# State-space stage: skip term and residual additions in TensorE's open sums, copies on ScalarE, delta projection in two halves

## What is computed

```
x1  = layernorm(x + attn(x))                    # attn's last product: o @ wo
z   = x1
u   = silu(conv4(in_proj(ctx_1024)) + conv_b)   # (b, channel, t)
dt, Bm, Cm = split(x_proj(u))                   # 16, 16, 16 rows
delta = softplus(dt_proj(dt) + dt_proj_b)
for t: state = state * exp(delta_t * A) + (delta_t * u_t) * B_t ;  y_t = state . C_t
y   = (y + D * u) * silu(z)                     # D * u is the skip term
x2  = layernorm(x1 + y)
out = layernorm(x2 + ffn(x2))
```

## Time and profile before

| | |
|---|---|
| median of 3 runs | 4593.2 us (4591.05 to 4596.53) |
| the profiled execution's own time | 4590.23 us |
| its span, and mean granted TensorE clock | 4588.4 us, 0.957 |
| state-space stage's main loop | first scan 3086.0, last sum ends 3784.5 us |
| its tail | gate 3785.4, last x2 copy ends 3809.5 us |
| busy over the span | PE 4184.2, DVE 3306.2, ACT 2299.2, POOL 963.4 us |

### The profile page before, as it was taken

The page is one execution under the profiler, slowest core; times in us unless marked ns, Lnnn a source line. Parts: engine busy times, 40 slices in busy tenths (PEclk is TensorE's granted clock), DMA queues, the critical chain, the costliest instruction groups (busy, mean ns, idle before and its releaser), DMA issues. The chain is left out here.

```text
span 4588.4 us, 184268 instructions
## 1 busy us (share of the span) xinstructions
PE 4184.2 (91%) x76786; PEld 2616.5 (57%) x76786; DVE 3306.2 (72%) x5635; ACT 2299.2 (50%) x5544; POOL 963.4 (21%) x1800
## 2 busy tenths in 40 slices
PE   6899999999999999999999999859778777999999
PEld 4576666666666766666666766633333333444443
DVE  2788887888887887888888888739999992222211
ACT  2566666665666665666666666544353431111110
POOL 0333333332323232333333233200000000000000
PEclk9899999999999999999999999878889887999999
DMA  1211212121212122121212212123233323000000
GB/s 52 65 57 60 73 47 73 53 66 54 70 57 64 56 64 62 57 70 56 67 56 67 62 59 71 50 102 83 72 99 83 86 79 148 0 28 28 0 19 9
DMA packets 131632, 277.95 MB, mean 61 GB/s; under 512 B 20668, under 2 KB 62032, under 8 KB 127200
## 3 DMA queue, kind: packets, MB, share of 16 engines
q1 hardware_dynamic: 126176, 258.29, 18.4%
q10 hardware_dynamic: 4608, 7.60, 0.5%
HBM read 235.17 MB, written 30.67 MB: 58 GB/s over the span
## 5 line engine op out<-in xcount | busy, mean ns | idle before, releaser
L504 PE MATMUL a_pb<-a_x_t,a_w_qkv 128*128 128x512 f32 x1536 | 838.2, 638 | 12.6 <-DMA a_w_qkv<-in_w_qkv 12.1
L1176 DVE TENSOR_TENSOR a_nq<-a_nq,a_tot 128x512 f32<-128x512 f32 x768 | 509.6, 705 | 151.0 <-PE a_pb L526 101.5
L1152 DVE SCALAR_TENSOR_TENSOR a_acc<-a_pb,a_taps,a_acc 128x511 f32<-128x511 f32 (+2 forms) x576 | 425.0, 738 | 41.4 <-ACT a_acc L847 10.7
L1778 PE MATMUL m_p_y<-m_h,m_ident 128*128 128x512 f32 x512 | 292.4, 686 | 143.2 <-DVE m_h L1978 143.2
L526 PEld LDWEIGHTS a_pb<-a_nq,a_ks 128*32 128x32 f32 x20480 | 215.5, 112 | 213.1 <-issue 117.9
L2246 PE MATMUL f_pb<-f_x_t,f_w_gu 128*128 128x512 f32 x704 | 308.0, 592 | 0.0
L526 PE MATMUL a_pb<-a_nq,a_ks 128*32 128x32 f32 x20480 | 253.0, 201 | 49.2 <-DVE a_nq L1313 31.8
L1464 POOL COPY a_apt<-a_apt_fine 32x256 f32<-32x256 f32 x256 | 100.8, 394 | 936.9 <-DVE a_apt_fine L1197 912.1
L504 PEld LDWEIGHTS a_pb<-a_x_t,a_w_qkv 128*128 128x128 f32 x1536 | 239.7, 191 | 96.0 <-issue 59.7
L1972 DVE TENSOR_TENSOR_SCAN m_h<-m_da,m_h 128x2048 f32<-128x2048 f32 x64 | 283.1, 4424 | 5.9
L2300 ACT ACTIVATE f_gate<-f_pb 128x512 f32<-128x512 f32 x132 | 78.8, 597 | 410.9 <-PE f_pb L2246 274.6
(11 more groups left out here) (278 smaller groups left out, 9153.1 us busy)
## 6 DMA issues: line engine op xcount, KB each, us to landing
a_rows<-rows SPq DMA_DIRECT2D x192, 512.0 KB, 3.9
a_amp_sums<-amp_sums SPq DMA_DIRECT2D x64, 508.0 KB, 3.6
attn_o<-a_o_t SPq DMA_DIRECT2D x64, 256.0 KB, 2.6
m_b_rows<-ssm_bc SPq DMA_DIRECT2D x64, 256.0 KB, 3.7
m_c_rows<-ssm_bc SPq DMA_DIRECT2D x64, 256.0 KB, 4.6
m_o_t<-attn_o SPq DMA_DIRECT2D x14, 1024.0 KB, 8.6
a_w_qkv<-in_w_qkv SPq DMA_DIRECT2D x51, 256.0 KB, 3.0
f_w_gu<-in_w_gu SPq DMA_DIRECT2D x3, 1536.0 KB, 17.9
```

The lines of the kernel that those rows point to most:

```text
L504: mm = nc.tensor.matmul(pb[:, V_BANK if i == P_V else KQ_BANK], w_qkv[:, i, k], x_t[:, k, b * T:(b + 1) * T], start=(k == 0), stop=(k == D ...
L1152: last = nc.vector.scalar_tensor_tensor(acc[:, i, d:T], src[:, 0:T - d], taps[:, i, 3 - d:4 - d], acc[:, i, d:T], ALU.mult, ALU.add)
L1176: last = nc.vector.tensor_tensor(part, part, spread(blocks, shape), ALU.mult)
L1778: nc.tensor.matmul(p_y[:, et], ident[:], h[:, (b * DS + n) % 3, et], start=(n == 0), stop=(n == DS - 1), skip_group_check=True).then_inc(s ...
```

## The change

1. Skip term: `finish` is gone. Four 128x128 diagonal matrices `diag_d` are built once (`build_diag`, VectorE, batch 0, step 1). Each tile of `p_y` is opened by a product diag_d x u, and the state sums are added to it. `gate` reads p_y itself, so p_y may be opened for the next batch only after the gate.
2. Attention residual: `p_o` is opened by ident x sums (the x rows), the heads are added, and ScalarE copies p_o to `sums` (`keep_o`). TensorE therefore waits for the x rows' DMA at step 0.
3. Gated residual: `p_turn` is opened by ident x x1, the four turns are ordinary products that add to it, and ScalarE copies the bank back to x1 (`keep_gated`).
4. Preparation: x_proj at TensorE's step 33, dt_proj in two halves at 38 and 42; on ScalarE 36, 40, 44, 47, 50; DU on VectorE at 54.
5. `x_dbl` lies in the first tile of `tap`, and `y_out` is gone.

```
-        U, DBL, DT, SOFT_EXP, SOFT_LOG, DU = range(ET, ET + 6)
-        PE_STEPS = {4 + 6 * et: et for et in range(ET)} | {31: DBL, 36: DT}
-        ACT_STEPS = {8 + 6 * et: et for et in range(ET)} | {30: U, 35: DBL, 40: DT, 43: SOFT_EXP, 46: SOFT_LOG}
-        DVE_STEPS = {8 + 6 * et: et for et in range(ET)} | {49: DU}
+        PE_STEPS = {4 + 6 * et: et for et in range(ET)} | {33: DBL, 38: DT_LOW, 42: DT_HIGH}
+        ACT_STEPS = {8 + 6 * et: et for et in range(ET)} | {30: U, 36: DBL, 40: DT_LOW, 44: DT_HIGH, 47: SOFT_EXP, 50: SOFT_LOG}
+        DVE_STEPS = {8 + 6 * et: et for et in range(ET)} | {54: DU}
...
 def project(b, tt, head):            # TensorE
+                        if tt == 0:
+                            pe.wait_ge(x_in, 16 * (b + 1))
+                        nc.tensor.matmul(p_o[:], ident[:], sums[:, tt], start=True, stop=False, skip_group_check=True)
-                    mm = nc.tensor.matmul(p_o[:], o_t[:, q % 2, head], w_o[:, head], start=(head == 0), stop=(head == H - 1),
+                    mm = nc.tensor.matmul(p_o[:], o_t[:, q % 2, head], w_o[:, head], start=False, stop=(head == H - 1),
...
 def turn_gated(b, lt):
+                        pe.wait_ge(x1_ready, b + 1)
+                    nc.tensor.matmul(p_turn[:], ident[:], x1[:, lt], start=True, stop=False, skip_group_check=True)
-                        mm = nc.tensor.transpose(p_turn[:, et * P:(et + 1) * P], gated[:, et, lt * P:(lt + 1) * P], ident[:])
+                        mm = nc.tensor.matmul(p_turn[:, et * P:(et + 1) * P], gated[:, et, lt * P:(lt + 1) * P], ident[:],
+                                              start=False, stop=(et == ET - 1), skip_group_check=True)
...
 def sum_state(j):
-                    if n == 0 and b:
-                        pe.wait_ge(y_ready, (b - 1) * ET + et + 1)
+                    if n == 0:
+                        if et == 0 and b:
+                            pe.wait_ge(gated_ready, b)
+                        if b == 0:
+                            pe.wait_ge(diag_ready, ET)
+                        pe.wait_ge(du_ready, b + 1)
+                        nc.tensor.matmul(p_y[:, et], diag_d[:, et], u[:, b % 2, et], start=True, stop=False, skip_group_check=True)
...
 ScalarE, at step i:
+                        if i % O_SPAN == O_SPAN - 1 and i < TT * O_SPAN:
+                            keep_o(b, i // O_SPAN)
+                        if b and i - TURN_G - 2 in (0, 2, 4, 6):
+                            keep_gated(b - 1, (i - TURN_G - 2) // 2)
...
+                def keep_o(b, tt):
+                    act.wait_ge(o_sum, b * TT + tt + 1)
+                    nc.scalar.copy(sums[:, tt], p_o[:]).then_inc(o_added, 1)
+                def keep_gated(b, lt):
+                    act.wait_ge(g_turned, b * TT + lt + 1)
+                    nc.scalar.copy(x1[:, lt], p_turn[:]).then_inc(g_added, 1)
...
 def gate(b):                         # VectorE
-                    dve.wait_ge(y_ready, b * ET + ET)
-                    nc.vector.tensor_tensor(gated[:], y_out[:], gated[:], ALU.mult).then_inc(gated_ready, 1)
+                    dve.wait_ge(summed, b * N + N)
+                    nc.vector.tensor_tensor(gated[:], p_y[:], gated[:], ALU.mult).then_inc(gated_ready, 1)
```

More of the change, by code:

```diff
@@ L1726, in prepare @@
                         pe.wait_ge(convolved, b * ET + ET)
-                        for et in range(ET):
+                        for et in range(2) if step == DT_LOW else range(2, ET):
                             if et >= 2:
@@ L1819, in prepare @@
                         act.wait_ge(projected, b * ET + et + 1)
+                        if et == 0 and b:
+                            act.wait_ge(dbl_stored, 16 * b)
                         if b >= 2:
@@ L1830, in prepare @@
                         act.wait_ge(dbl_sum, b + 1)
-                        if b:
-                            act.wait_ge(dbl_stored, 16 * b)
-                        nc.scalar.copy(x_dbl[:], p_d).then_inc(dbl_ready, 1)
+                        nc.scalar.copy(x_dbl, p_d).then_inc(dbl_ready, 1)
                         act.wait_ge(dbl_ready, b + 1)
                         act.dma_start(io["ssm_bc"][b], x_dbl[DR:, :]).then_inc(dbl_stored, 16)
-                    elif step == DT:
+                    elif step in (DT_LOW, DT_HIGH):
                         soft, linear = delta[:, b % 2], du[:, b % 2]
-                        for et in range(ET):
+                        for et in range(2) if step == DT_LOW else range(2, ET):
                             act.wait_ge(dt_sum, b * ET + et + 1)
@@ L1926, in _ @@
                             keep_x2_t(b - 1, (i - TURN_X - 3) // 3)
+                for lt in range(TT):
+                    keep_gated(B - 1, lt)
                 deviation(2 * B - 1)
@@ L1979, in times_c, with build_diag @@
                                             ALU.mult).then_inc(cs_ready, 1)
-                def finish(b):
+                def build_diag():
+                    dve.wait_ge(weights, 80)
                     for et in range(ET):
-                        dve.wait_ge(summed, b * N + N - ET + et + 1)
-                        nc.vector.scalar_tensor_tensor(
-                            y_out[:, et], u[:, b % 2, et], cols[:, et, 6:7], p_y[:, et],
-                            ALU.mult, ALU.add).then_inc(y_ready, 1)
-                def add_o(b, tt):
-                    if tt == 0:
-                        dve.wait_ge(x_in, 16 * (b + 1))
-                    dve.wait_ge(o_sum, b * TT + tt + 1)
-                    nc.vector.tensor_tensor(sums[:, tt], sums[:, tt], p_o[:], ALU.add).then_inc(o_added, 1)
+                        nc.vector.tensor_scalar(diag_d[:, et], ident[:], cols[:, et, 6:7], None, ALU.mult).then_inc(diag_ready, 1)
                 def moments(q, src):
-                    dve.drain()
+                    b, second = divmod(q, 2)
+                    dve.wait_ge(g_added if second else o_added, (b + 1) * TT)
                     for i in range(TT):
@@ L2017, in gate @@
                     dve.wait_ge(z_ready, b + 1)
-                    dve.wait_ge(y_ready, b * ET + ET)
-                    nc.vector.tensor_tensor(gated[:], y_out[:], gated[:], ALU.mult).then_inc(gated_ready, 1)
-                def add_gated(b, lt):
-                    dve.wait_ge(x1_ready, b + 1)
-                    dve.wait_ge(g_turned, b * TT + lt + 1)
-                    nc.vector.tensor_tensor(x1[:, lt], x1[:, lt], p_turn[:], ALU.add).then_inc(g_added, 1)
+                    dve.wait_ge(summed, b * N + N)
+                    nc.vector.tensor_tensor(gated[:], p_y[:], gated[:], ALU.mult).then_inc(gated_ready, 1)
                 for step in DVE_STEPS.values():
@@ L2035, in _ @@
                             scan(row)
-                        if b and i == FINISH:
-                            finish(b - 1)
+                        if i == 1 and b == 0:
+                            build_diag()
                         if et == 1 and row:
@@ L2044, in _ @@
                             prepare(b + 1, step)
-                        if i % O_SPAN == O_SPAN - 1 and i < TT * O_SPAN:
-                            add_o(b, i // O_SPAN)
                         if i == NORM_1:
@@ L2052, in _ @@
                             gate(b - 1)
-                        if b and i - TURN_G - 2 in (0, 2, 4, 6):
-                            add_gated(b - 1, (i - TURN_G - 2) // 2)
                         if b and i == NORM_2:
@@ L2059, in _ @@
                 times_c(B * DS - 1)
-                finish(B - 1)
                 gate(B - 1)
-                for lt in range(TT):
-                    add_gated(B - 1, lt)
                 moments(2 * B - 1, x1)
```

13 lines of the change are left out of this document (7 added, 6 removed).

## The result

The changed kernel takes 4602.7 us (median of 15 runs, 4591.0 to 4611.7) beside 4589.9 us for the kernel before on the same chips (15 runs, 4582.7 to 4597.8): a ratio of 1.0026, 95% interval 1.0017 to 1.0036. It is 12.7 us slower; the forecast was 13.7 us slower.

What follows compares the result with a forecast made beforehand. VectorE was taken as the bound, with TensorE close behind. The terms 12.4 - 1.8 - 2.1 - 0.3 + 5.5 = +13.7 us, on the median 4593.2, gave 4607 us, range 4590 to 4620.

Steps and rivals of the forecast that it cites:

- Openings: First steps of each batch: 2.6, 3.5, 2.0 and 4.3 us longer, together +12.4, ends +9 to +18.
- The three waits: Opening of batch 1: VectorE waits 3.2 us at step 7, 3.4 at step 11 and 2.5 at step 12.
- rival (c): Clock falls in the new waits; openings, loaded stretches and tail at their high ends: +26 us, 4619 us, chance 0.14.
- Scan of step 12: Opening of batch 1: the scan waits 2.5 us for decay 15, queued behind ACT's copy of the first turn.
- Steps 32 to the end: Loaded stretch, forecast as steps 29 to 52: -0.7 us in each of batches 0 to 2, -0.3 in batch 3.
- waits by product count: Loaded stretch, batches 0 to 2: VectorE waits 1.6, 3.6, 1.3 and 1.5 us at steps 35, 39, 47 and 51.
- Tail: After the last sum: four turns, two at 4.4 us and two at 2.65; +5.5 us together, ends +1.9 and +9.
- Steps 17 to 29: VectorE alone decides; one add less in batches 0 to 2 gives -1.8 us.
- batch 3's small terms: Steps 29 to 52 of batch 3: one product more (+0.9 us), two adds fewer (-1.2), so -0.3.
- Rival (a): VectorE's relief comes through, not held up by TensorE's and ACT's queues: -25 us, 4568 us, chance 0.15.

Runs made afterwards that it cites:

- e5: The changed kernel with the x rows added to p_o after the 16 heads instead of before them: stage 747.2 us, ratio 1.0035.
- e3: The changed kernel with VectorE's gate ahead of times B in step 7 instead of behind it: stage 733.5 us, ratio 1.0009.
- e4: The changed kernel with the skip product added at state row 13 instead of opening the sum: stage 730.5 us, ratio 1.0005.
- e6: The changed kernel with ScalarE's four copies of p_turn one step later (11, 13, 15, 17): stage 737.6 us, ratio 1.0013.
- e10: The changed kernel with the moves of e3, e4 and e6 together, x rows not moved: stage 718.1 us, ratio 0.9970.
- e9: The changed kernel with the moves of e3, e4 and e6, and the x rows last in the first token tile only: stage 710.2 us, ratio 0.9946.
- e1: The kernel before with only the new preparation steps (x_proj 33, dt_proj halves 38 and 42, delta's operations 54): stage 730.5 us, ratio 0.9997.
- e2: The changed kernel with the old preparation steps (x_proj 31, dt_proj whole at 36, delta's operations at 49): stage 747.2 us, ratio 1.0045.
- e7: The changed kernel with true transposes, no x1 product, and the gated adds back on VectorE: stage 749.5 us, ratio 1.0040.
- e11: As e9, with the 16 heads of a token tile spread over 12 steps instead of 9: stage 749.0 us, ratio 1.0031.

## Why the prediction was right, and where its terms were not

Direction, size and mechanism were right: 13.7 us against 12.7 in the runs and 13.2 in the stage. The work that VectorE shed came back as its waits for TensorE. That the sum came within a microsecond is mostly luck, as the openings were 8.1 us too low and the other terms 8.6 too high together. Point by point:

- **Openings.** The three waits are where they were put. e5 takes away the one at step 7, e3 and e4 together the one at step 11, and e6 the one at step 12. The sum was too small by 8 us, and above the +18 given as its end. The step that failed is "VectorE needs ... 8.8 us until times B of step 11, which wants just that sum: 3.4 us of wait": it had TensorE go on at full clock after the 2 us wait for the gate, and rival (c) was told against with "the wait for the gate is 2 us". In this order the clock did fall behind it: 5.3 instead of 3.4 us of wait in batch 1, 7.6 instead of 5.7 in batch 3, and e3 shows 2.0 and 1.9 us of them to be the clock's. The length of the wait does not settle it, for in e5 the same wait has full clock behind it; the early place of the x rows has a part in it. Likewise "batches 2 and 3 TensorE enters at full clock, so the first wait is 1.7": with the x rows' wait before it, it enters at half clock, and the waits are 3.0 and 3.4. Batch 0, without gate or DMA wait, was right (2.6, measured 2.4). e10 against e9 gives the x rows 4.5 us in the openings, near the 1.7 us of later start that the count had for each.
- **Scan of step 12.** 2.5 forecast, 2.34 measured three times; e6 removes 2.24.
- **Steps 32 to the end.** The waits by product count were each right to 0.5 us. The -0.7 per batch was a middle between -1.8 and +0.4, according to the second fall of the clock, after dt_proj. It did not come in any batch, and no run with dt_proj in halves has it, so the count without it was the one to take. Measured were -2.6, -0.8 and -2.5. The first fall explains the spread: in batches 0 and 2 the change has one fall less than the kernel before, 1.8 us each by the clock, in batch 1 as many. Taken off, -0.8, -0.8 and -0.7 are left, so the term without that luck was near the forecast and 1 us short of the count's -1.8. The forecast's remark that the stretch also lost two adds is not enough for it: over batches 0 to 2 the split alone gives -0.2 (e1), the rest of the change without it -1.9 (e2 against before), both together -5.9.
- **Tail.** Each turn at full clock was forecast at 2.65 and measured 2.69. The choice of two turns at each level was wrong: all four ran at full clock, and the term is +1.9, its low end. The Trainium skill's rule, put beside the sum, gave that value; the sum had not gone by it. Nor was it certain: in four later runs with this tail the first turn was at half clock.
- **Steps 17 to 29** and batch 3's small terms: within 0.8 us.

So 8.1 us too little in the openings stand against 5.0 too much in the rest of the batches and 3.6 too much in the tail. The total owes its closeness to that. Most of each error is the clock's: it fell behind the gate where it had been taken as full, was full in the tail where half had been allowed for, and fell less often at the start of the loaded stretches than in the kernel before.

Rival (a), that VectorE's relief comes through, did not come: the order of events stood against it, and e9 shows what it takes. The same instructions in other places give 33.7 us of stage back. e7 and e11 show the limit.

## What to carry to other kernels

When work is moved from the bound engine to one that idles, ask at which places in its queue it lands: here the change, with 48 more products of 0.86 us, cost 13 us of stage in its first order and gained 20 in another, with nothing added or taken away. An open sum took its extra term at its start, at its end (e5) and at row 13 (e4): put it where the engine waits anyway, and put the reader of a bank that must be emptied ahead of work that does not need it. A copy handed to an engine with time to spare is free only if what it waits for is done when it comes up, since everything behind it waits too. And before an edit is credited with a few microseconds, compare the granted clock in both traces stretch by stretch: here one fall more or less is 1.7 us.

## What was not expected of the hardware

How long TensorE waits does not tell what clock it finds. Behind the gate's wait of 2.08 us it was at half (0.68 over the next 5.4 us) in batches 1 and 2, which made that wait cost 4.08 us; in e5, without the x rows' wait some 15 us earlier, the same wait had 1.00 behind it. After 7.2 us of idling it was at half as well (e4). In the tail a wait of 2.45 us was followed by full clock in the change and by half clock in e6, with the same instructions behind it; ordinary products then came back to full clock within a turn, transposes stayed at half through all four (e7). What parts these cases no run here shows. One fall where TensorE is scarce costs as much as two products, 1.7 us.
